# A sandwich block (latent attention, then ternary FFN) on one core: TensorE's order of a chunk rewritten around the last down products

## What is computed

```python
h = layernorm(x)
Q, V = h @ Wq.T + bq, h @ Wv.T + bv              # 16 heads of 32
logits = einsum("bhtd,lhd->bhtl", Q, latent) / sqrt(32)   # 64 latent keys per head
top4 = top_k(logits, 4); w = softmax(top4)
attn = (sum of w * the chosen latents) + V
x = x + layernorm(attn @ Wo.T + bo)
up, gate = layernorm(x) @ wu.T, layernorm(x) @ wg.T       # 512 -> 2048
x = x + layernorm((silu(up) * gate) @ wd.T)               # 2048 -> 512
```

## Time and profile before

| | |
|---|---|
| median of 3 runs | 1192.83 us |
| the profiled execution | 1190.24 us |
| its span, first to last instruction | 1188.5 us |
| TensorE (PE) busy | 1024.9 us, 86% |
| VectorE (DVE) busy | 786.9 us, 66% |
| ScalarE (ACT) busy | 517.3 us, 44% |
| GpSimd (POOL) busy | 457.0 us, 38% |
| mean granted TensorE clock | 0.939 |
| DMA, 16 engines | 25% |

### The profile page before, as it was taken

The page is one execution under the profiler, slowest core; times in us unless marked ns, Lnnn a source line. Parts: engine busy times, 40 slices in busy tenths (PEclk is TensorE's granted clock), DMA queues, the critical chain, the costliest instruction groups (busy, mean ns, idle before and its releaser), DMA issues. The chain is left out here.

```text
span 1188.5 us, 17411 instructions
## 1 busy us (share of the span) xinstructions
PE 1024.9 (86%) x5428; PEld 474.2 (40%) x5428; DVE 786.9 (66%) x2781; ACT 517.3 (44%) x793; POOL 457.0 (38%) x374
## 2 busy tenths in 40 slices
PE   2522597999899998999899989999899999998997
PEld 1322243444444444444444434444444444433443
DVE  6499775975488376965498466965597468927333
ACT  4478355533444424534444434524454444432330
POOL 1138232642255333633256233633256234632230
PEclk7755698999899999999899999999999999999999
DMA  7832331123301231123301321123202320112000
GB/s 227 324 103 36 71 54 54 36 43 83 89 18 36 71 77 48 36 53 77 83 18 36 88 63 44 36 53 84 76 18 53 85 58 18 28 45 45 9 1 36
DMA packets 152449, 74.62 MB, mean 63 GB/s; under 512 B 136768, under 2 KB 136768, under 8 KB 151360
## 3 DMA queue, kind: packets, MB, share of 16 engines
q1 hardware_dynamic: 152384, 73.95, 25.2%
HBM read 31.99 MB, written 8.39 MB: 34 GB/s over the span
## 5 line engine op out<-in xcount | busy, mean ns | idle before, releaser
L578 PE MATMUL ug<-X1T,TU 128*128 128x512 f16 x1024 | 248.7, 387 | 26.9 <-DVE ugt L1200 22.6
L578 PE MATMUL ug<-X1T,TG 128*128 128x512 f16 x1024 | 242.6, 380 | 0.0
L983 POOL TENSOR_TENSOR hT<-ugt,hT 128x512 f16<-128x512 f32 x128 | 148.0, 1156 | 207.9 <-ACT hT L821 206.9
L588 PE MATMUL ring<-TD,hT 128*128 128x512 f16 x1024 | 225.7, 379 | 1.8 <-POOL hT L983 1.8
L578 PEld LDWEIGHTS ug<-X1T,TU 128*128 128x128 f16 x1024 | 97.5, 99 | 156.7 <-DVE ugt L1200 38.0
L814 ACT ACTIVATE ugt<-ug,cu 128x512 f32<-128x512 f32 x128 | 87.4, 683 | 165.2 <-PE ug L578 165.2
L588 PEld LDWEIGHTS ring<-TD,hT 128*128 128x128 f16 x1024 | 99.1, 98 | 125.5 <-POOL hT L983 5.2
L578 PEld LDWEIGHTS ug<-X1T,TG 128*128 128x128 f16 x1024 | 100.4, 98 | 121.9 <-issue 1.9
L1195 DVE SCALAR_TENSOR_TENSOR ugt<-ugt,ug 128x512 f32<-128x512 f32 x128 | 86.9, 679 | 86.8 <-ACT ugt L814 86.8
L970 POOL TENSOR_TENSOR Lb<-Lb,v 128x1024 f32<-128x1024 f32 x32 | 82.6, 2582 | 74.0 <-DVE Lr L1232 67.3
L1232 DVE MATCH_REPLACE8 Lr<-v,Lb 128x68 f32<-128x68 f32 x512 | 102.3, 213 | 0.0
(11 more groups left out here) (170 smaller groups left out, 1545.8 us busy)
## 6 DMA issues: line engine op xcount, KB each, us to landing
x_in<-in_L_attn_hidden_states SPq DMA_DIRECT2D x8, 1024.0 KB, 4.8
out_dram<-Lr SPq DMA_DIRECT2D x32, 256.0 KB, 3.3
x<-in_L_attn_hidden_states SPq DMA_DIRECT2D x28, 256.0 KB, 3.5
hT<-in_L_ffn_W_up SPq DMA_DIRECT2D x8, 512.0 KB, 7.5
hT<-in_L_ffn_W_down SPq DMA_DIRECT2D x8, 512.0 KB, 4.3
TD<-in_L_ffn_W_gate SPq DMA_DIRECT2D x4, 512.0 KB, 11.7
TU<-in_L_attn_Wq SPq DMA_DIRECT2D x1, 1024.0 KB, 7.5
TG<-in_L_attn_Wv SPq DMA_DIRECT2D x1, 1024.0 KB, 9.1
```

The source lines that it names most:

```text
L578: last = pe.matmul(ug[:, 2 * (e % 2) + s, :], w[:, k, e * P:(e + 1) * P], X1T[:, b, k, :], start=(k == 0 and b == 0), stop=(k == KD - 1 an ...
L588: last = pe.matmul(ring[:, bank, :], hT[:, a, e, t * P:(t + 1) * P], td[:, e, :], start=(e == 0 and a == 0), stop=(e == NE - 1 and a == 1))
L983: pool.tensor_tensor(hT[:, 1, e, :], ugt[:, 2 + e % 2, :], hT[:, 0, e, :], ALU.subtract).then_inc(h_lo, 1)
```

## The change

- TensorE's order of a mid body becomes: Q, upgate blocks 0 and 1 in token halves (both blocks for tokens 0 to 255, then both for 256 to 511), logits 0 and 1, upgate 2 to 6, logits 2, upgate 7 to 10, logits 3, upgate 11 to 15, V 0 and 1, down 0, down 1, V 2 and 3, the weighted latents of all heads (`weigh`), down 2, WO 0 to 3, down 3. In the last body: V 0, V 1, down 0, V 2, V 3, `weigh`, down 1, WO 0 to 3, down 2, down 3.
- `down(t)` writes `ug` bank t instead of a ring bank; it waits for `hidden` of block 14 (t < 2) or 15. `upgate(1)`'s first half waits until all four down banks of the chunk before have been read.
- `weigh` has no zero padding: 48 matmuls of 64 rows to 32 columns (512 tokens each), in four column strips and two row halves, for the 24 of 128 rows to 64 columns.
- The FFN's rows are evicted by ACT (scale and shift, `f_rows`), and POOL adds the residual (`f_out`). Tile 3 is DVE's instead (`f_row`), with the residual from a copy `x1_kept`, so that its x1 rows can be reloaded early in the next body; POOL adds the shift (`f_shift`).
- `low_q(3)`, and in mid bodies `s1_lo`, move from DVE to POOL. `f_a` has one tensor_scalar fewer.
- `select(3)` and `probs_lo(2)` move behind the last block, and each `select`, `shift` and `normalise` stands one to three blocks later than before.
- SP's transposes `t2` of tiles 2 and 3 move to the end of the body that makes their rows; XT may be overwritten once V is computed.

The diff, cut to its core:

```diff
+def ring_jobs(kind):
...
+    return q + lg + v + wo
...
                 if ffn and att:
-                    t2(-1, 2)
-                    t2(-1, 3)
...
+                def weigh(a):
+                    banks = [plan[("VW", 0, 2 * a + s)][0] for s in range(2)]
...
+                        wait(pe, p_t, i, 16 * TT, 16 * TT)
...
+                    for n, (b, c) in enumerate(((0, 0), (0, 1), (1, 0))):
+                        for r in range(4):
+                            for s in range(2):
+                                rows = slice(64 * s, 64 * s + 64)
+                                last = pe.matmul(ring[32 * r:32 * r + 32, banks[s], :], latV[b][rows, 4 * a + r, :],
+                                                 PT[rows, c, 4 * a + r, :], start=False, stop=(n == 2), skip_group_check=True)
...
-                def upgate(e):
+                def upgate(e, half=None):
+                    cols = slice(0, CH) if half is None else slice(half * 2 * P, half * 2 * P + 2 * P)
+                    if e == 0 and half is not None:
                         for s in range(2):
-                            wait(pe, x1_t[s], j, 32, 32)
+                            wait(pe, x1_t[s], j, 32, 16 * half + 16)
+                    if e == 1 and half == 0:
+                        wait(pe, f_sum, j, TT, 0)
...
                 def down(t):
-                    bank = bank_of("DN", -1, t)
+                    wait(pe, h32_ready, j, NE, NE - 1 if t < 2 else NE)
...
-                            last = pe.matmul(ring[:, bank, :], hT[:, a, e, t * P:(t + 1) * P], td[:, e, :],
+                            last = pe.matmul(ug[:, t, :], hT[:, a, e, t * P:(t + 1) * P], td[:, e, :],
...
-                for e in range(NE):
+                for half in range(2):
+                    upgate(0, half)
+                    upgate(1, half)
+                for e in range(2, NE):
+                    if att and e == 2:
+                        logits(0, 1)
                     upgate(e)
-                    if att and e == 5:
+                    if att and e == 6:
                         logits(2)
-                    if att and e == 9:
+                    if att and e == 10:
                         logits(3)
-                down(0)
-                down(1)
...
+                    v(0)
+                    v(1)
+                    down(0)
+                    if kind == "mid":
+                        down(1)
+                    v(2)
+                    v(3)
+                    weigh(0)
+                    weigh(1)
+                    down(2 if kind == "mid" else 1)
+                    for t in range(TT):
+                        wo(t)
+                    if kind == "last":
+                        down(2)
+                    down(3)
...
+                def keep_residual():
+                    wait(act, x1_ready, i, TT, 0)
+                    wait(act, f_sum, j, TT, 0)
+                    act.activation(x1_kept[:, :], x1[:, TT - 1, :], ACT.Copy).then_inc(kept, 1)
...
+                def f_rows(t):
+                    wait(act, f_bias, j, TT, t + 1)
+                    wait(act, out_stored[(t + 2) % 4], j, 16, 16 if t >= 2 else 0)
+                    act.activation(out_buf[t % 2], ug[:, t, :], ACT.Identity, scale=rcf[:, t % 2:t % 2 + 1],
+                                   bias=nbf[:, t % 2:t % 2 + 1]).then_inc(f_sum, 1)
...
+                def f_out(t):
+                    wait(pool, f_sum, j, TT, t + 1)
+                    pool.tensor_tensor(out_buf[t % 2], out_buf[t % 2], residual(kind == "tail")[:, t, :],
+                                       ALU.add).then_inc(out_ready, 1)
...
+                AFTER = {0: [], 1: [(maxes, 0, 0), (maxes, 0, 1)],
+                         2: [(slots, 0), (replace, 0, 0)], 3: [(replace, 0, 1), (sums, 0)],
+                         4: [(maxes, 1, 0), (maxes, 1, 1)], 5: [(slots, 1), (select, 0)],
+                         6: [(replace, 1, 0)], 7: [(replace, 1, 1), (sums, 1)],
+                         8: [(probs_lo, 0), (maxes, 2, 0)], 9: [(maxes, 2, 1), (select, 1)],
+                         10: [(slots, 2), (replace, 2, 0)], 11: [(replace, 2, 1), (sums, 2)],
+                         12: [(probs_lo, 1), (maxes, 3, 0)], 13: [(maxes, 3, 1), (select, 2)],
+                         14: [(slots, 3), (replace, 3, 0)], 15: [(replace, 3, 1), (sums, 3)]}
```

More of the change, by code:

```diff
@@ L49 @@
 TINY = 2.0 ** -100
[L51 to L58, removed]
-    if kind == "first":
[L60 to L82, removed]
-def ring_plan(kind):
[L87 to L98, removed]
+def ring_jobs(kind):
+    if kind == "tail":
+        return []
+    q = [("Q", 0, m) for m in range(KD)]
+    v = [("VW", 0, m) for m in range(KD)]
+    wo = [("WO", 0, t) for t in range(TT)]
+    lg = [("L", 0, n) for n in range(2 * TT)]
+    if kind == "first":
+        wt = [("WT", 0, n) for n in range(3 * KD)]
+        return wt[:4] + q + lg[:4] + wt[4:] + lg[4:] + v + wo
+    return q + lg + v + wo
+def ring_plan(kind):
+    jobs = ring_jobs(kind)
+    before = [] if kind == "first" else [("WO", -1, t) for t in range(TT)]
+    seq = before + jobs
+    at = len(before)
+    return {job: (n % 4, seq[n + at - 4] if n + at >= 4 else None) for n, job in enumerate(jobs)}
 def build(nc, x, Wq, bq, Wv, bv, Wo, bo, lat, Wu, Wg, Wd, out):
@@ L431, in body @@
                         s1(t)
-                if kind == "last":
+                if ffn and nxt:
+                    reload(2)
+                    out(2)
+                if att:
                     for t in range(TT):
                         t2(0, t)
-                if ffn and nxt:
-                    reload(2)
-                if ffn:
+                if ffn and not nxt:
                     out(2)
-                if nxt:
-                    t2(0, 0)
-                    t2(0, 1)
-                if ffn and nxt:
-                    reload(3)
                 if ffn:
@@ L1049, in body @@
                     rstd_f(2)
+                    f_out(2)
+                if ffn:
                     rstd_f(3)
+                if ffn and nxt:
+                    f_shift(3)
+                elif ffn:
+                    f_out(3)
             bodies(pool, body)
@@ L1431, in body @@
                     y_c(0, 1)
+                    y_a(3)
                     t2_lo(0, 0)
-                if nxt:
-                    f_a(3)
+                    y_b(2)
                     t2_lo(0, 1)
-                    f_b(3)
-                    y_b(2)
-                    y_a(3)
-                    y_c(0, 2)
-                    y_b(3)
-                    t2_lo(0, 2)
-                if kind == "last":
-                    y_a(3)
-                    t2_lo(0, 1)
-                    y_b(2)
                     y_b(3)
                     y_c(0, 2)
+                    y_c(0, 3)
+                if ffn and nxt:
+                    f_a(3)
+                if att:
                     t2_lo(0, 2)
-                    y_c(0, 3)
+                if ffn and nxt:
+                    f_b(3)
+                    f_row(3)
+                if att:
                     t2_lo(0, 3)
                 if not nxt:
-                    for t in (2, 3):
-                        f_a(t)
-                        f_b(t)
+                    f_a(2)
+                    f_b(2)
+                    f_a(3)
+                    f_b(3)
             bodies(dve, body)
```

293 lines of the change are left out of this document (149 added, 144 removed).

## The result

The changed kernel takes **1119.3 us** (median of 4 runs, 1116.61 to 1121.47), against 1192.76 us for the kernel before in the same comparison: a ratio of 0.938, 95% interval 0.936 to 0.940. The time was forecast at 1098, its main case at 1090 to 1106, with a range up to 1124. The sign and the cause hold, and of a forecast gain of 94.8 us, 73.5 came. The time lies outside the main case. It lies inside the range, but that is in part luck: the range was widened for rivals 1 to 3, which took some 2 us at most. The time was lost in the two ends, and for these the forecast had 5 us of doubt in the first body and none in the others.

What follows compares the result with a forecast made beforehand. TensorE was taken to bound the kernel, through its work, idle time and half clock. Span 1188.5 - 78.6 (six periods) - 9.5 (first body) - 6.9 (last body) + 0.2 (tail) = 1093.7, hence 1098 us; range up to 1124.

Steps and rivals of the forecast that it cites:

- main case: Whole kernel: TensorE bound with at most a microsecond of waits per period, 1090 to 1106 us, chance 0.55.
- what is late next is X1T of tiles 2 and 3: Mid seam, second token halves: the last transpose lands at 62.0 against 63.7, slack 1.6 us, no wait taken.
- I take 0 for the waits of this phase: Upgate phase: TensorE never waits for DVE's `hidden`; the ends were 0 and the present 4.0 us.
- with joints 0.3: Steady period: 0.3 us for joints, added to 113.9, 2.7 and 1.5 to give 118.4 us.
- -9.5: First body: its phase ends at 240.1 instead of 249.56, a gain of 9.5 us, give or take 5.
- the prediction's own rule for moved work: Operations moved to POOL, about 10 us per period, cost nothing as long as `low_a` follows at once on ACT.
- The tail starts at once: End of last body: down 3 ends at 52.9 and the tail follows without a gap, -6.9 us for the last body.
- Rival 4: Seam: `f_row(3)` and the work behind it finish late, holding `upgate(1)` and logits; slower than before, about 1225 us, chance 0.03.
- +0.2: Tail: ACT and POOL finish the last rows instead of DVE and ACT, one tensor_scalar fewer, 0.2 us more.
- Rival 1: `weigh`: the eight tiles don't run together, so it takes 2.8 or 5.4 us; 1107 or 1125 us, chance 0.10.
- rival 3: Upgate phase: DVE and POOL have no slack and contention is passed on, six or seven times 4 us; 1124, chance 0.11.
- Rival 2: Seam: X1T's tile 3, PT or V's low halves come 2 to 4 us late, six times; 1110 to 1122, chance 0.17.

Runs made afterwards that it cites:

- the two undone parts: Changed kernel with logits 0 and 1 back directly behind Q: 1148.22 us; separately, changed kernel with upgate blocks 0 and 1 computed whole: 1149.65 us.
- the last version: Changed kernel with `low_q(3)` before the all-reduce, `f_a(2)` earlier, tail block 0 whole first, `weigh(0)` behind V 1, last body's `probs_lo(3)` before `f_a(0)`: 1108.08 us.
- the second experiment: Changed kernel with `f_a(2)` ahead of the last low half in the last body, and the tail computing block 0 whole before block 1: 1112.91 us.
- the first experiment: Changed kernel with POOL making the low half of Q's slice 3 before its second all-reduce in the first body: 1116.75 us.

## Why the prediction was right, and where it was off

**The seam** was forecast by its mechanism and came so: no wait of the logits, none for `hidden` in the phase, and the two undone parts lose 4.2 and 5.5 us a period. The 7.0 us that were put to the logits' new place are too many for it alone: put back, it costs 4.2, and what took the rest of the old gap away no run undid by itself. The step "what is late next is X1T of tiles 2 and 3" named the right successor. Its term was mis-sized twice: the last `t2_lo` takes 1.41 us and not 0.6, and the landing is 3.1 to 4.2, not 3.0. Slack 0.5 to nothing, not 1.6.

**The phase.** "I take 0 for the waits of this phase" holds exactly, and the reason given for it, `select` two blocks behind its `replace`, is shown by the run that puts it back, together with ACT's exp. That POOL would be as tight as DVE didn't come true in waits, though `hidden_lo` is 14% dearer than the row that the layout was made from.

**`weigh`** at 1.5 measured 1.42; the other end, 5.4, is excluded. By the Trainium skill's ratio for nine tiles (TensorE: Matmul & The Clock Gate, Measured speedup vs the span model), carried over to eight, it would have been an estimated 1.85. Here 48 matmuls of 0.2158 take 1.42, a speedup of 7.3 on eight places: the trace is better than that ratio. What the prediction cites on the fast weight load stands on its page under Restrictions, not under Performance Considerations; 48 weight loads pass within these 1.42 us.

**The period** of 118.4 measured 119.2, or 118.88 where X1T doesn't wait and some 119.5 where it does. The difference of 0.5 in the undisturbed one is in the joints: one of about 0.1 stands around each of the logits and `weigh`, and a half matmul is 0.109. The term "with joints 0.3" was too small. TensorE busy at 95% and a clock of 0.97 were named as signs; they came at 89% and 0.955, and are means over the whole span, on which the first body weighs. The 95% could not have come: TensorE's 995.2 us are 91% even of the forecast span.

**The first body**, -9.5 "give or take 5", was +2.0. This is the step that failed, in two terms. The first is `low_q(3)`'s move to POOL, taken for one operation of 1.16 us without asking what it is moved past. The all-reduce stands there in the code, and the prediction's own rule for moved work was applied to DVE and ACT but not to POOL's queue in the one body with another order. The run that turns the two round gives 4.1 of the 6.2 us ahead of L1126 back. Of what is left then, 1.3 us are a later start of that execution, seen already at POOL's first low half (44.97 for 43.63). In the last version that start is as early as before, L1126 is 1.7 late, and the all-reduce 1.4 late, with one more low half in front of it. The second term is the 2.4 us for the wait for PT. The wait was real and is gone, but the body didn't wait for TensorE there: with it the stretch to `y_a(0)` took 31.4 us, without it and without the four evictions in a row 31.6. The four evictions cost 1.0. That DVE's ternary pieces are the pace was forecast; that they were the pace already was not. Of the last 1.7 us 1.0 is the second halves, which take 5.7 us at a granted clock of 0.60, for 4.7.

**The last body and the tail.** The wait for PT of 3.0 was forecast and is 2.92. "The tail starts at once" is right for block 0 and wrong for block 1. Rival 4 had the place and the mechanism, `f_row(3)` behind other work on DVE and upgate(1) waiting for it, but its price was worked out only for the mid seams, where `f_row(3)` ends at 58.2 us (forecast 57.1, wanted at 61.9). In the last body `f_a(2)` stands behind `t2_lo(3)`, and the tail has no logits or `low_q` for which to go first. The term "+0.2" missed 7.8, 5.0 of which the edit gives back. That `upgate(1)` in the tail is as late is a wait that the prediction put at nothing there. **Rival 1** (eight tiles don't run together) and **rival 3** (the phase stays DVE's) are excluded. **Rival 2** (the seam ends late) came true in three seams with half a microsecond, not with 2 to 4. Rival 4's 1225 doesn't come out of its own terms: seven seams of 15 and 2.2 us give 1218; nothing rests on it.

**Not undone by themselves** were the downs' new banks, the eviction of the FFN's rows by ACT with POOL's addition, and the kept residual. What each is worth isn't shown.

## What to carry to other kernels

When a step is moved to another engine, read that engine's queue in every variant of the loop, first and last bodies too: here the steady period was right to 0.8 us, and the two ends missed 21. A wait of TensorE that is taken away gives nothing back where another engine sets the pace: 5.9 us went, and the body was no shorter. A wait can be bought away by putting independent work before it, but each new order names the next late operand; ask for its landing, not its issue. And a table of work on an engine that is 85% full in its phase needs its own layout: one place in it was worth 15 us.

## What the hardware showed that was not expected

- **An all-reduce on POOL costs its queue 13 to 15 us, not 0.37.** 7.80 us of issue lie ahead of it and 7.48 behind it; in the run with the other order 6.26 and 7.00, in the kernel before 6.82 and 6.92. Its operand was made at 44.26, 11.5 us before it starts. The Trainium skill (GPSIMD Engine Reference, Instruction dispatch) says that the first call of a freshly loaded kernel pays about 6 us with no instruction to see; the size is near. Whether code loading is what fills this time no run here shows.
- **DVE beside POOL.** DVE's last low half of a seam (512 columns) takes 1.40 to 1.56 us in the six mid seams, where POOL works on 512 columns as well, and 0.69 in the first and the last body, where POOL does nothing at that moment. No run took POOL's work away. The Trainium skill (GPSIMD Engine Reference, Key points) has the two share their interfaces to SBUF where DVE reads two tensors from it, which this one does.
- **Which gap brings half clock isn't told by its length.** The wait for PT of 2.9 us in the last body is followed by `weigh` at 0.51 of the clock in the changed kernel (2.7 us for it) and at full clock in the second experiment; a gap of 2.36 before the tail's second halves left the clock at 1.00 there, and one of 2.34 at the same place of the last version was followed by some 3 us at half. The same wait for PT in the first experiment left `weigh` at full clock, and the down behind it ran partly at half (8.53 us for 7.08). With the logits in front, six seams have the same gap of 2.5 to 2.7 us: in four the clock stayed at 1.00 for the 4 us behind it, in the other two it was 0.79 and 0.59. The gaps of 4 and 5 us quoted above were each followed by half clock. What decides between them stays open.
- **X1T's transposes are issued in 1.23 us and land 3.1 to 4.2 us after issue**, and the spread of one microsecond is as large as all of the seam's slack.
